# Eighteen rows padded to 128 in the products that spread the gates of a gated mixture

## The reference

```python
def _L1_ffn_ref(x, gate_w, experts_gate_up, experts_down, shared_gate_w, shared_up_w, shared_down_w, shared_expert_gate_w):
    logits = x_flat @ gate_w.T
    scores = jax.nn.softmax(logits, axis=-1)
    _, topk_ids = jax.lax.top_k(scores, NUM_EXPERTS_PER_TOK)           # 2 of 8
    in_topk = jax.nn.one_hot(topk_ids, E, dtype=x.dtype).sum(axis=1)
    w = scores * in_topk
    gu = jnp.einsum('nh,eih->nei', x_flat, experts_gate_up)
    g, u = (gu[..., :I], gu[..., I:])                                  # I = 176
    h = jax.nn.silu(g) * u
    expert_out = jnp.einsum('nei,ehi->neh', h, experts_down)
    out = jnp.einsum('neh,ne->nh', expert_out, w)
    shared = jax.nn.silu(x_flat @ shared_gate_w.T) * (x_flat @ shared_up_w.T) @ shared_down_w.T
    shared_weight = jax.nn.sigmoid(x_flat @ shared_expert_gate_w.T)
    out = out + shared_weight * shared
    ...
x = x + 0.5 * _L1_ffn_ref(_layernorm(x, axis=-1), ...)
```

## Time and profile before

| | |
|---|---|
| time, median of 3 runs | 2476.32 us (2476.25 to 2477.66) |
| profiled execution, its own time | 2477.06 us |
| its span, first to last instruction | 2475.2 us |
| PE busy | 2028.7 us, 82% of the span |
| PEld busy | 1569.4 us, 63% |
| DVE busy | 1398.8 us, 57% |
| ACT busy | 958.4 us, 39% |
| POOL busy | 134.7 us, 5% |
| granted clock of PE, mean | 0.868 of full speed |

### The profile page before, as it was taken

One profiled execution on the slowest core, in us unless ns is written; L12 is line 12 of the kernel. 1 busy time (PEld: TensorE's weight loads), 2 busy tenths in 40 slices (PEclk: granted clock), 3 DMA queues, 4 the chain that ended last, 5 costly groups with the idle time before them and its releaser, 6 DMA issues. The chain is left out here.

```text
span 2475.2 us, 38219 instructions
## 1 busy us (share of the span) xinstructions
PE 2028.7 (82%) x13180; PEld 1569.4 (63%) x13180; DVE 1398.8 (57%) x3614; ACT 958.4 (39%) x2141; POOL 134.7 (5%) x193
## 2 busy tenths in 40 slices
PE   3588788669977883999899999999799985887875
PEld 2355455358963223898899867878699973555543
DVE  6654455655558997555422247676622238555547
ACT  1345444331213330221444355555344444334444
POOL 1100000110001002000000000000000000000000
PEclk9779788769989995899899999999799988566668
DMA  5000000000000000000000034444100000000000
GB/s 143 25 1 1 1 1 1 30 3 1 0 1 0 0 0 16 22 1 0 1 0 0 20 102 128 138 127 133 52 1 0 0 1 0 1 1 0 0 1 17
DMA packets 47225, 60.05 MB, mean 24 GB/s; under 512 B 7112, under 2 KB 44712, under 8 KB 46510
## 3 DMA queue, kind: packets, MB, share of 16 engines
q1 hardware_dynamic: 47122, 58.73, 7.7%
HBM read 32.51 MB, written 26.21 MB: 24 GB/s over the span
## 5 line engine op out<-in xcount | busy, mean ns | idle before, releaser
L757 ACT ACTIVATE m2a_hid<-psum,m_b 128x256 f32<-128x256 f32 x256 | 100.2, 474 | 113.8 <-PE psum L55 113.7
L757 ACT ACTIVATE m2b_hid<-psum,m_b 128x256 f32<-128x256 f32 x256 | 100.2, 474 | 113.5 <-PE psum L55 113.4
L742 PE MATMUL psum<-m_w,m2a_hid 128*128 128x128 f32 x1024 | 125.5, 276 | 0.0
L742 PE MATMUL psum<-m_w,m2b_hid 128*128 128x128 f32 x1024 | 125.4, 276 | 0.0
L775 DVE SCALAR_TENSOR_TENSOR m2b_acc<-psum,m2b_gates,m2b_acc 128x128 f32<-128x128 f32 x128 | 39.0, 346 | 147.2 <-PE psum L742 147.2
L775 DVE SCALAR_TENSOR_TENSOR m2a_acc<-psum,m2a_gates,m2a_acc 128x128 f32<-128x128 f32 x128 | 39.0, 346 | 147.2 <-PE psum L742 147.2
L742 PEld LDWEIGHTS psum<-m_w,m2a_hid 128*128 128x128 f32 x1024 | 121.5, 193 | 0.6
L742 PEld LDWEIGHTS psum<-m_w,m2b_hid 128*128 128x128 f32 x1024 | 121.4, 193 | 0.6
L2147 ACT ACTIVATE a_p<-a_p,a_nmax 128x256 f32<-128x256 f32 x128 | 64.0, 500 | 142.7 <-DVE a_nmax L2171 142.7
L1878 DVE TENSOR_REDUCE a_nmax<-psum 128x2 f32<-128x512 f32 x128 | 82.7, 686 | 48.7 <-PE psum L1719 48.5
L1112 DVE TENSOR_TENSOR_SCAN a1s_clamped<-a1s_clamp_coef,a1s_bounds 128x1024 f32<-128x1024 f32 x48 | 108.7, 2266 | 0.0
(11 more groups left out here) (623 smaller groups left out, 5454.8 us busy)
## 6 DMA issues: line engine op xcount, KB each, us to landing
a_scratch<-a_pos SPq DMA_DIRECT2D x64, 384.0 KB, 2.7
a_shifted<-a_scratch SPq DMA_DIRECT2D x64, 256.0 KB, 3.1
m_w<-in_m_w SPq DMA_DIRECT2D x1, 2048.0 KB
arena<-in_m_w SPq DMA_DIRECT2D x1, 2048.0 KB, 8.8
arena<-in_m_up SPq DMA_DIRECT2D x1, 1792.0 KB, 7.1
a_w<-in_a_w SPq DMA_DIRECT2D x1, 1536.0 KB, 7.6
out<-X SPq DMA_DIRECT2D x1, 1024.0 KB, 5.1
m_down<-in_m_down SPq DMA_DIRECT2D x1, 896.0 KB, 4.4
```

The lines of the kernel that those rows point to most:

```text
L742: last = nc.tensor.matmul(ps_y(e % 2)[:, t * D:(t + 1) * D], hid[:, e % 2, c * SEQ + t * P:c * SEQ + (t + 1) * P], m.m2_w2[:, e, c, :], st ...
L757: last = nc.scalar.activation(hid[:, e % 2, c * SEQ:(c + 1) * SEQ], ps_up(e % 2)[:, c * SEQ:(c + 1) * SEQ], ACT.Gelu, bias=m.m2_b1[:, e * ...
```

## The change

`parts_T` and `pick` get 128 partitions instead of 18. The array of `pick` that comes from the host is padded with zero rows to 128, so the load and the cast on POOL have 128 rows. A new memset on POOL, ahead of the cast, sets all of `parts_T` to zero and increments a new semaphore, `cleared`; ACT and DVE wait for it before they copy the turned gates into the first 18 rows. The `spread` matmuls, whose text does not change, then contract over 128 rows, of which 110 are zero in both operands. The order of instructions on PE, ACT, DVE and SP stays as it is.

```diff
-        parts_T = sb("parts_T", [OWNERS, NB * SEQ], F32R)
-        pick = sb("pick", [OWNERS, 2 * S * P], F32R)
-        raw_pick = m.arena[0:OWNERS, 2, 0:2 * S * P]
+        parts_T = sb("parts_T", [P, NB * SEQ], F32R)
+        pick = sb("pick", [P, 2 * S * P], F32R)
+        raw_pick = m.arena[:, 2, 0:2 * S * P]
...
-        pick_loaded, pick_ready = sem("pick_loaded"), sem("pick_ready")
+        pick_loaded, pick_ready, cleared = sem("pick_loaded"), sem("pick_ready"), sem("cleared")
...
                 if k == 1:
+                    act.wait_ge(cleared, 1)
                     for g in (0, 2):
                         act.wait_ge(turned, g + 1)
-                        nc.scalar.activation(parts_T[:, g * 512:(g + 1) * 512], m.psum[0:OWNERS, TURN_BANK[g], :],
+                        nc.scalar.activation(parts_T[0:OWNERS, g * 512:(g + 1) * 512], m.psum[0:OWNERS, TURN_BANK[g], :],
                                              ACT.Copy).then_inc(even_moved, 1)
...
+            dve.wait_ge(cleared, 1)
             for g in (1, 3):
                 dve.wait_ge(turned, g + 1)
-                nc.vector.tensor_copy(parts_T[:, g * 512:(g + 1) * 512], m.psum[0:OWNERS, TURN_BANK[g], :]).then_inc(odd_moved, 1)
+                nc.vector.tensor_copy(parts_T[0:OWNERS, g * 512:(g + 1) * 512], m.psum[0:OWNERS, TURN_BANK[g], :]).then_inc(odd_moved, 1)
...
         def _(pool):
+            nc.gpsimd.memset(parts_T[:, :].bitcast(F32), 0.0).then_inc(cleared, 1)
             pool.wait_ge(pick_loaded, 16)
             nc.gpsimd.tensor_copy(pick[:, :], raw_pick).then_inc(pick_ready, 1)
...
-    arrays["m1_pick"] = (np.arange(18)[:, None] % 9 == np.minimum(np.arange(14 * P) // 176, 8)[None]).astype(np.float32)
+    pick = (np.arange(18)[:, None] % 9 == np.minimum(np.arange(14 * P) // 176, 8)[None]).astype(np.float32)
+    arrays["m1_pick"] = np.pad(pick, ((0, P - 18), (0, 0)))
```

## The result

The changed kernel takes 2441.44 us in the median of four runs (2435.24 to 2444.7), against 2476.99 (2476.25 to 2478.21) before: a ratio of 0.9846, with a 95% interval of 0.9826 to 0.9867. It is faster by 1.5%, inside the range and 6.6 us above the forecast. The profiled execution took 2443.27 us, with a span of 2441.4.

What follows compares the result with a forecast made beforehand. PE was taken to bound m1a and m1b, with weight loads held back around the 18-row spreads. 108 steps at 0.384 us give 41.5 us: 2477.06 to 2435.6, less 0.74 for the median, 2434.8 us; range 2431 to 2445.

Steps and rivals of the forecast that it cites:

- the range: Whole kernel's median time: 2431 to 2445 us, holding most of the full gain's 0.90 chance.
- What bounds the stage, and that it is the rows: Steady m1a and m1b: PE sets the pace, and weight loads lag when the number of rows changes, 0.384 us a step.
- 0.384 us a step, 108 steps: Steps of m1a and m1b: each gives back 0.384 us, 54 steps in each of two stages, 41.5 us.
- the four starts: Each step, line 55's matmul to line 54's: two spreads, lines 53 and 54, 0.86 us shrinking to 0.476.
- the sum: Gain counted from the steps of the two gated stages, m1a and m1b: 41.5 us.
- A padded matmul as line 54's, 0.119: Spread matmuls in the steps: padded to 128 rows, each costs 0.119 us, not line 736's 0.22.
- the half gain: Rival, spread in the steps: padded matmul costs 0.22 us, so 21.8 us gained, time 2456.6; chance 0.05.
- No other engine late: Steps of m1a and m1b: DVE's tightest chain keeps 1.65 us spare, so PE stays the bound.
- POOL: Starts of m1a and m1b: memset 1.9 to 5.6 us, cast 1.67 to 4.9 us; cost taken as nothing.
- The rule of the Trainium skill that weight loads overlap only across row groups: Spread's weight loads: by this rule padding changes nothing, time stays at 2476.3 us; chance 0.02 within no gain's 0.03.
- the sentence that the stages ahead, between and after should last as before: Stages outside m1a and m1b: expected to last unchanged in the profile after.
- the allowance for POOL's cast: Routing on DVE at the stages' starts: a cast meeting it costs up to 4.9 us twice, setting the range's high end.

Runs made afterwards that it cites:

- E1: The changed kernel with 64 rows in place of 128 in parts_T, pick and its load: 2474.44 us, 0.9998 of the kernel before.
- E2: The changed kernel with 65 rows in place of 128 in parts_T, pick and its load: 2428.34 us, 0.9825 of the kernel before.
- E5: The changed kernel plus three unread 512-column DVE multiplications at the end of m1b, delaying m2a: 2437.26 us.
- E6: The kernel before plus two unread DVE multiplications (512 and 256 columns) at the end of m1b: 2488.14 us against 2480.75, 1.003.

## Why the prediction came out as it did

- *What bounds the stage, and that it is the rows:* right. The loads wait at the change between a part of the array's rows and all of them; E1 and E2 put the boundary between 64 and 65.
- *0.384 us a step, 108 steps:* the four starts shrank by 0.38, a step by 2.94 - 2.57 = 0.37, which is 40 us for 108. (The 0.59 shown, over five, is 0.118 a start; 0.119 comes from the starts to the nanosecond.) The two stages gave 45.5. The rest lies at the stages' starts: before, the third step of m1a took 4.46 us and that of m1b 5.28, for the most part at the lower clock (its `down` in m1b is the earlier trace rows); after, both take 2.55, at the full clock, which is 3.9 us beyond the 0.37 each. The clock at m1a's third step, before, after, and with 65 rows:

```profile
560.20:563.40 3.20, 3.20 (x15) 2.98 (x15) 1.51 (x3) 0.50 (x1) 0.00 (x0) 0.50 0.00 0
```

```profile
557.00:563.40 6.40, 4.66 (x40) 4.48 (x39) 4.62 (x7) 1.12 (x3) 0.00 (x0) 1.00 0.00 0
```

```profile
555.40:558.60 3.20, 3.20 (x17) 3.20 (x16) 1.81 (x3) 0.60 (x1) 0.00 (x0) 0.50 0.00 0
```

With 65 rows the third steps took 4.11 and 4.68 us, and the two stages gave 41.4 us, which is the sum. So the surplus came with the stages' starts and not with the steps; it was not in the sum, and what decides it was not tested.
- *A padded matmul as line 54's, 0.119:* right, two in 639.96 - 639.72 = 0.24, so not the half gain.
- *No other engine late:* right; PE is busy for 137.0 of 137 us in both loops.
- *POOL:* the memset took 1.80 us (1.9 estimated), the cast 1.96 and 2.12. The cast again holds up DVE, now at the fourth subtraction and not the first, and again where PE has the logits to do, so the routing was not hit. In m1b it was close: DVE was through at 974.03, PE's logits at 974.09. The lines of m1a:

```profile
534.44 1.80 POOL L688 MEMSET m1a_parts_T<- 128x2048 f32 x1 [6.84 <-POOLq L78]
539.08 1.96 POOL L690 CAST m1a_pick<-arena 128x1792 fp32r<-128x1792 f32 x1 [2.84 <-DMA arena<-in_m_pick]
```

```profile
539.79 1.79 DVE L423 TENSOR_TENSOR m1a_XT_low<-m1ar_XT,m1a_XT_high 128x512 fp32r<-128x512 f32 x1 [0.29 <-ACT m1a_XT_high L407]
544.79 0.31 DVE L428 COPY m1ar_logits<-psum 128x144 f32<-128x144 f32 x1 [3.20 <-PE psum L390]
```

- *The rule of the Trainium skill that weight loads overlap only across row groups* ("TensorE: Matmul & The Clock Gate", Part 3): the runs speak against it. With 128 rows the load of line 575 starts with the matmul of line 55, at 639.60, and in the loops loads run beside matmuls on the same rows all the time: PEld is busy for 136.79 of 137 us, and with 65 rows for 127 of 127.
- *The step that failed* is the sentence that the stages ahead, between and after should last as before. They took 11.7 us more in the profiled execution, 7.2 of them in m2a and the attention behind it, and this ate the 4 us of surplus and some 7 us of the gain. The term for it stood at nothing. E5 and E6 show these two as a matter of where m2a starts: PE comes out of the idle stretch ahead of it at 1.2 GHz (0.50), and whether its first serial work gets 2.4 GHz in time turns on a microsecond or two. That the 4 us of surplus made up for a part of the loss was luck: without them the median would have come out near 2445.4, past the range's end.
- *The range:* its low end leaned on three runs of before within 1.4 us. In later batches before ran from 2466.42 to 2490.97 us. The scatter was larger than those three runs showed, and the 2441 stayed inside through the allowance for POOL's cast, that is, for a reason that did not occur.

## What to carry to other kernels

A short contraction among full ones (18 or 64 rows among 128 here) costs a weight load that is held back on the way in and on the way out, 0.37 us for both here; read it as idle time of the weight loader ahead of two lines, and fill the rows with zeros past 64, if the operands can be zeroed off the critical path. A gain in the middle of a kernel shifts every later stage; where stages begin with serial work on a PE that has been idle, allow for some microseconds either way per such start, or keep PE busy over the idle stretch.

## What the runs showed that was not expected

Sixty-four rows and 65 differ by 0.38 us a switch pair, with nothing in between: 0.86 against 0.48 us for the same four starts. Idle time made stages shorter by more than itself: 2.3 us of delay took 4.3 us out of m2a and 2.5 out of the attention behind it (E5). Whether the whole kernel became faster is not shown, since its ratio to before, 0.9822 (0.9797 to 0.9848), overlaps with that of the change, 0.9846. And 1.2 us of delay made m2a 4.3 us longer in the kernel before, which was 7.4 us slower in the median (E6).
